# A two-layer vision transformer tower on one core: the random-feature attention computes its angles in row blocks of 32

## The reference, cut to what matters

```python
H, Dh, m = 16, 16, 64
Q, K, V = heads(wq), heads(wk), heads(wv)
def _phi(x, rf, m):
    proj  = einsum('bhtd,md->bhtm', x, rf)
    scale = exp(-sum(x * x) * 0.5) / sqrt(m)
    return concatenate([cos(proj), sin(proj)]) * scale
Qf, Kf = _phi(Q), _phi(K)
KV  = einsum('bhnd,bhnv->bhdv', Kf, V)
QKV = einsum('bhnd,bhdv->bhnv', Qf, KV)
Z   = maximum(Qf . sum(Kf), 1e-06)
h = h + (QKV / Z) @ wo.T
```

## Time and profile before

| | |
|---|---|
| median of three runs | 464.89 us (464.15 to 467.36) |
| the profiled execution | 466.66 us, span 464.8 us |
| TensorE busy (PE) | 377.4 us, 81% |
| VectorE (DVE) | 238.3 us, 51% |
| GpSimd (POOL) | 184.2 us, 40% |
| ScalarE (ACT) | 171.3 us, 37% |
| mean granted clock of TensorE | 0.899 |

### The profile page before, as it was taken

One profiled execution on the slowest core, in us unless ns is written; L12 is line 12 of the kernel. 1 busy time (PEld: TensorE's weight loads), 2 busy tenths in 40 slices (PEclk: granted clock), 3 DMA queues, 4 the chain that ended last, 5 costly groups with the idle time before them and its releaser, 6 DMA issues.

```text
span 464.8 us, 9446 instructions
## 1 busy us (share of the span) xinstructions
PE 377.4 (81%) x3380; PEld 319.6 (69%) x3380; DVE 238.3 (51%) x798; ACT 171.3 (37%) x403; POOL 184.2 (40%) x97
## 2 busy tenths in 40 slices
PE   5999999988169999999707999999983199999930
PEld 4878888876159898999607758777772187887730
DVE  2834434352425455555336054577867267676713
ACT  1264343430113434353302565554421145345410
POOL 0016510101250989999063900012114117687524
PEclk9999999995559999999956999999995589999985
DMA  8999200000016878883525000000000147887313
GB/s 303 414 430 420 93 11 13 13 12 24 19 31 223 301 284 301 292 300 114 198 69 204 1 0 1 1 1 23 1 23 11 62 114 260 271 269 240 121 32 119
DMA packets 16352, 65.34 MB, mean 141 GB/s; under 512 B 2880, under 2 KB 8512, under 8 KB 11584
## 3 DMA queue, kind: packets, MB, share of 16 engines
q1 hardware_dynamic: 14784, 60.72, 35.8%
q0 software_dynamic: 1536, 4.20, 2.9%
HBM read 55.21 MB, written 9.70 MB: 140 GB/s over the span
## 4 chain that ended last, share of the span: by engine, by line
PE 69%; ACT 8%; issue 7%; DVE 7%; DMA 5%; POOL 2%; SPq 0%; POOLq 0%; DVEq 0%; ACTq 0%
PE ps L695 10%; PE ps L697 9%; PE ps L696 9%; PE ps L1102 7%; PE ps L422 7%; PE ps L1113 3%; PE ps L455 3%; PE ps L1288 3%; PE ps L1125 3%; PE ps L475 2%; PE ps L1099 2%; PE ps L985 2%; POOL area_y L553 2%; ACT ps L508 2%; PE ps L598 1%
## 5 line engine op out<-in xcount | busy, mean ns | idle before, releaser
L695 PE MATMUL ps<-xeT,wslot 128*128 128x160 bf16 x384 | 84.2, 240 | 7.1 <-DVE xeT L760 3.3
L696 PE MATMUL ps<-xeT,wslot 128*128 128x160 bf16 x384 | 83.8, 239 | 0.0
L878 POOL TENSOR_TENSOR area_q<-wslot 128x4096 bf16<-128x4096 f32 x8 | 56.4, 7054 | 36.0 <-DMA wslot<-blob_dram 36.0
L884 POOL TENSOR_TENSOR area_w<-wslot 128x2048 bf16<-128x2048 f32 x16 | 57.6, 3602 | 10.9 <-DMA wslot<-blob_dram 10.9
L697 PE MATMUL ps<-xeT,area_q 128*128 128x160 bf16 x256 | 55.1, 238 | 0.0
L695 PE MATMUL ps<-hid,wslot 128*128 128x160 bf16 x256 | 53.7, 233 | 0.0
L697 PE MATMUL ps<-hid,area_w 128*128 128x160 bf16 x256 | 53.6, 233 | 0.0
L696 PE MATMUL ps<-hid,wslot 128*128 128x160 bf16 x256 | 53.5, 233 | 0.0
L695 PEld LDWEIGHTS ps<-xeT,wslot 128*128 128x128 bf16 x384 | 38.7, 101 | 13.8 <-issue 6.1
L772 DVE TENSOR_TENSOR hid<-ps,hid 128x160 bf16<-128x160 f32 x128 | 39.7, 316 | 1.1
L878 POOL TENSOR_TENSOR area_w<-wslot 128x2048 bf16<-128x2048 f32 x8 | 28.8, 3602 | 28.1 <-DMA wslot<-blob_dram 20.1
(11 more groups left out here) (169 smaller groups left out, 806.8 us busy)
## 6 DMA issues: line engine op xcount, KB each, us to landing
wslot<-blob_dram SPq DMA_DIRECT2D x8, 2048.0 KB, 7.7
wslot<-blob_dram SPq DMA_DIRECT2D x16, 1024.0 KB, 5.7
wslot<-blob_dram SPq DMA_DIRECT2D x8, 1031.0 KB, 5.2
slots_dram<-hid SPq DMA_DIRECT2D x8, 544.0 KB, 14.0
xe<-slots_dram SPq DMA_DIRECT2D x16, 128.0 KB, 2.1
slots_dram<-ye SPq DMA_DIRECT2D x16, 128.0 KB, 4.8
area_x<-x_dram SPq DMA_DIRECT2D x4, 384.0 KB, 6.3
area_w<-wq_dram SPq DMA_DIRECT2D x1, 1024.0 KB, 9.2
```

Of the source, the lines that this page charges most:

```text
L695: nc.tensor.matmul(out, w_high[:, s, high_at:high_at + P], x_high, start=first, stop=False)
L696: nc.tensor.matmul(out, w_high[:, s, high_at:high_at + P], x_low, start=False, stop=False)
L878: nc.gpsimd.tensor_tensor(w_low1[L][:, s, :], wslot[:, s, 0:SECOND[L]], w_high[:, s, 0:SECOND[L]], ALU.subtract).then_inc(main[L].low1_rea ...
L884: nc.gpsimd.tensor_tensor(w_low2[:, s, :], wslot[:, s, o:o + KF * D], w_high[:, s, o:o + KF * D], ALU.subtract).then_inc(main[L].low2_read ...
```

## The change

- The angles of eight heads (four `angles` steps) are computed by one group on TensorE: four blocks of 32 rows, each with two heads of 16 rows, each into its own bank (`F_BANK` = 1, 2, 6, 4). `rfs` has two places instead of eight. The quarter turn is a matmul of 32 rows with 1/32 of the value. The group waits until all earlier angle banks are taken. ScalarE and VectorE work per bank as before.
- Bank 4 now holds angles, so `kernel` has bank 3 alone and waits for the mask of the step before.
- ScalarE runs a small `Exp` once the first tile of the second attention is normed, and a small `Sin` right ahead of its first rounding copy.
- For tiles 0 and 1 (`EARLY`) VectorE keeps only the statistics of the `norm` step. `refine` and `norm_apply` run on GpSimd, and so does the scaling into `xin`.

```diff
+HT = 2
-        rfs = sb("rfs", [P, HC, P])
+        rfs = sb("rfs", [P, HT, P])
-        quarter = sb("quarter", [1, P], BF16)
-        ones_row = sb("ones_row", [1, 4 * P], BF16)
+        quarter = sb("quarter", [P, P], BF16)
+        ones_row = sb("ones_row", [P, 4 * P], BF16)
+        early = sb("early", [P, 2])
+        outer_guess = sem("outer_guess")
+        EARLY = NT - 2
...
         def project1_act(act):
+            act.wait_ge(ln_done[2], 1)
+            nc.scalar.activation(early[:, 0:1], const[:, C_ONE:C_ONE + 1], ACT.Exp)
...
-        F_BANK = (1, 2, 6)
+        F_BANK = (1, 2, 6, 4)
+        A_BANK = 3
+        QUARTERS = 4
...
                 if step == "angles":
                     t, j = n // 8, n % 8
-                    if n >= 3:
-                        pe.wait_ge(F_taken, n - 2)
-                    nc.tensor.matmul(ps[:, F_BANK[n % 3], :], quarter[:], ones_row[:], start=True, stop=False)
-                    for a in range(2):
-                        hd = 2 * j + a
-                        mm = nc.tensor.matmul(ps[:, F_BANK[n % 3], a * 2 * P:(a + 1) * 2 * P], rfs[:, hd % HC, :],
-                                              qkT1[:, t, hd // HC, :, :], start=False, stop=(a == 1))
-                    mm.then_inc(F_full, 1)
+                    if n % QUARTERS:
+                        continue
+
+                    if n:
+                        pe.wait_ge(F_taken, n)
+                    parts = [(F_BANK[b], slice(b * HT * DH1, (b + 1) * HT * DH1)) for b in range(QUARTERS)]
+                    for bank, r in parts:
+                        nc.tensor.matmul(ps[:, bank, :], quarter[r, :], ones_row[r, :], start=True, stop=False)
+                    for a in range(HT):
+                        for bank, r in parts:
+                            mm = nc.tensor.matmul(ps[:, bank, a * 2 * P:(a + 1) * 2 * P], rfs[r, a, :],
+                                                  qkT1[r, t, j // 4, :, :], start=False, stop=(a == 1))
+                            if a == 1:
+                                mm.then_inc(F_full, 1)
                 elif step == "kernel":
...
-                    if n >= 2:
-                        pe.wait_ge(A_taken, n - 1)
+                    if n:
+                        pe.wait_ge(A_taken, n)
...
         def attn1_act(act):
+            nc.scalar.activation(early[:, 1:2], const[:, C_BEFORE:C_BEFORE + 1], ACT.Sin)
...
                 elif step == "norm":
                     dve.wait_ge(wo_taken[1], n + 1)
-                    norm_tile(dve, st, n, h, xn, ln_done[3])
+                    if n < EARLY:
+                        norm_stats(dve, st, n, h, outer_guess)
+                    else:
+                        norm_tile(dve, st, n, h, xn, ln_done[3])
...
-                elif step == "xin":
-                    dve.wait_ge(rstd_ready, n + 1)
-                    norm_apply(dve, n, xn, xin, xin_ready)
+                elif step == "xin" and n >= EARLY:
+                    dve.wait_ge(rstd_ready, n - EARLY + 1)
+                    norm_apply(nc.vector, n, xn, xin, xin_ready)
...
             for t in range(NT):
+                if t < EARLY:
+                    pool.wait_ge(outer_guess, t + 1)
+                    refine(nc.gpsimd, newton[:, 1, :], own.step, t, own.step)
+                    norm_apply(nc.gpsimd, t, h, xn, ln_done[3])
                 pool.wait_ge(inner_guess, t + 1)
-                refine(nc.gpsimd, newton[:, 1, :], own.step, t, lambda ins: ins.then_inc(rstd_ready, 1))
+                if t < EARLY:
+                    refine(nc.gpsimd, newton[:, 1, :], own.step, t, own.step)
+                    norm_apply(nc.gpsimd, t, xn, xin, xin_ready)
+                else:
+                    refine(nc.gpsimd, newton[:, 1, :], own.step, t, lambda ins: ins.then_inc(rstd_ready, 1))
...
-            nc.vector.memset(quarter[:, FEAT:P], 0.25).then_inc(quarter_ready, 1)
+            nc.vector.memset(quarter[:, FEAT:P], 0.25 / (HT * DH1)).then_inc(quarter_ready, 1)
```

More of the change, by code:

```diff
@@ L120, in build @@
         w1 = sb("w1", [P, 4, KD, D])
-        rfb = sb("rfb", [P, HC, P])
-        rfs = sb("rfs", [P, HC, P])
+        rfb = sb("rfb", [P, HT, P])
+        rfs = sb("rfs", [P, HT, P])
         wslot = sb("wslot", [P, 2, W0])
@@ L234, in norm_stats, with norm_apply @@
                                     float(RSQRT_MAGIC), ALU.mult, ALU.add).then_inc(ready, 1)
-        def norm_apply(dve, t, src, dst, done):
-            nc.vector.tensor_scalar(dst[:, t, :], src[:, t, :], mv[:, t, 0:1], rstd[:, t:t + 1],
-                                    ALU.subtract, ALU.mult).then_inc(done, 1)
+        def norm_apply(eng, t, src, dst, done):
+            eng.tensor_scalar(dst[:, t, :], src[:, t, :], mv[:, t, 0:1], rstd[:, t:t + 1],
+                              ALU.subtract, ALU.mult).then_inc(done, 1)
         def refine(eng, work, step, t, done):
@@ L256, in norm_tile @@
             refine(nc.vector, newton[:, 0, :], st.step, t, st.step)
-            norm_apply(dve, t, src, dst, done)
+            norm_apply(nc.vector, t, src, dst, done)
         ln_done = [sem(f"ln_done{n}") for n in range(4)]
@@ L1031, in norm2_dve @@
                 for t in range(first, first + 2):
-                    norm_apply(dve, t, h, xn, ln_done[2])
+                    norm_apply(nc.vector, t, h, xn, ln_done[2])
         def values1_dve(dve, st):
@@ L1109, in attn1_pe @@
                     pe.wait_ge(feat_ready, 2 * n + 2)
-                    if n >= 2:
-                        pe.wait_ge(A_taken, n - 1)
+                    if n:
+                        pe.wait_ge(A_taken, n)
                     for a in range(4):
-                        mm = nc.tensor.matmul(ps[:, 3 + n % 2, a * P:(a + 1) * P], feat[:, 4 * g + a, 1, :],
+                        mm = nc.tensor.matmul(ps[:, A_BANK, a * P:(a + 1) * P], feat[:, 4 * g + a, 1, :],
                                               feat[:, 4 * g + a, 0, :], start=True, stop=True)
@@ L1159, in attn1_act @@
                         act.wait_ge(feat_ready, n - 2)
-                    nc.scalar.activation(vt[:, n % 3, :], ps[:, F_BANK[n % 3], :], ACT.Identity,
+                    nc.scalar.activation(vt[:, n % 3, :], ps[:, F_BANK[n % 4], :], ACT.Identity,
                                          bias=const[:, C_ROUND:C_ROUND + 1]).then_inc(whole_ready, 1)
@@ L1180, in attn1_dve @@
                     dve.wait_ge(whole_ready, n + 1)
-                    nc.vector.scalar_tensor_tensor(vt[:, n % 3, :], vt[:, n % 3, :], ROUND, ps[:, F_BANK[n % 3], :],
+                    nc.vector.scalar_tensor_tensor(vt[:, n % 3, :], vt[:, n % 3, :], ROUND, ps[:, F_BANK[n % 4], :],
                                                    ALU.subtract, ALU.subtract).then_inc(F_taken, 1)
@@ L1186, in attn1_dve @@
                         dve.wait_ge(av_done, n - 1)
-                    nc.vector.tensor_tensor(am[:, n % 2, :, :], ps[:, 3 + n % 2, :].rearrange("p (a n) -> p a n", a=4),
+                    nc.vector.tensor_tensor(am[:, n % 2, :, :], ps[:, A_BANK, :].rearrange("p (a n) -> p a n", a=4),
                                             image, ALU.mult).then_inc(A_taken, 1)
@@ L1356 @@
     patches = patches.reshape(NT, P, KP, P).transpose(3, 0, 2, 1).reshape(P, NT, KP * P)
-    rf = np.zeros((P, HC, P), np.float32)
+    rf = np.zeros((P, HT, P), np.float32)
     for j in range(HC):
         for twice in range(2):
-            rf[j * DH1:(j + 1) * DH1, j, twice * FEAT:(twice + 1) * FEAT] = np.asarray(L1_attn_rf).T
+            rf[j * DH1:(j + 1) * DH1, j % HT, twice * FEAT:(twice + 1) * FEAT] = np.asarray(L1_attn_rf).T
     arrays = {
```

## The result

The changed kernel takes 474.91 us in the median (472.29 to 475.58), the kernel before 464.89: the ratio is 1.018, 95% interval 1.013 to 1.023. It is slower; 459.8 was predicted, with 468 as the upper end. Medians here are of all executions of a kernel, but every ratio leaves out executions over 1.5% above the fastest of their kernel, so that it can differ a little from the ratio of the medians.

What follows compares the result with a forecast made beforehand. TensorE's matmuls were taken to bound the second attention; 10.5 us gained at full clock less 5.4 lost to the clock gave 5.1 net, from the median of 464.89 to 459.8 us, range 453.5 to 468.

Steps and rivals of the forecast that it cites:

- The clock takes part of it back: Second attention and tail: TensorE's clock falls at the two waits for GpSimd, taking 5.4 of the 10.5 us gained.
- My walk: Walk along the engine queues through the eight angle groups of the second attention, summed at full clock to 64.05 us.
- 5.0 of 6.4 us in the plain groups: TensorE's work within each plain angle group; full clock was expected in groups 1 and 2.
- In a stretch without pauses it rises again: TensorE's clock recovers under unbroken work, read from a mean of 0.79 at 114 to 116 us.
- my term: The clock's predicted cost: 2.2 us each in groups 5 and 7 and 1 in the tail, 5.4 together.
- The slower rival: Low clock sets in with group 3 and never rises: 4.5 us slower, 469.4 us; chance 0.13.
- a cold group leaves TensorE hardly a pause: Argument against the slower rival: at the lower clock a group has 10.5 us of TensorE work, which is the bound.
- About nothing: Worth of moving the norms to GpSimd: 2.5 us Newton steps and 0.6 scaling there, against 2.07 on VectorE.
- G = 1.4: TensorE's time in us for the angles of eight heads, four row blocks at once; bounds 1.25 and 5.5.
- The chain of one group: Group of four angle steps, TensorE through ScalarE's copies to VectorE's last subtraction: 6.4 us, against 9.1 before.
- The divide's place: Group 3, where VectorE's divide of 1.25 us is queued between subtractions: the group takes 7.35 us.
- the tables: ScalarE's early Exp and Sin table loads: about 1 us gained together, all in group 0.

Runs made afterwards that it cites:

- the set g: One of four sets of kernels, each on one chip beside the kernel before; the changed kernel took 473.17 there against 465.1, ratio 1.014.
- The two filled kernels: Changed kernel with useless matmuls in TensorE's pauses, norms of two tiles on GpSimd (461.62 us) or all on VectorE (455.35), against 467.21 for the kernel before.
- the filled kernel with them on GpSimd: Changed kernel plus useless matmuls in TensorE's pauses, norms of tiles 0 and 1 on GpSimd: 461.62 us, ratio 0.989 to the kernel before; first measured 460.32, 0.987.
- the filled kernel with norms on VectorE: Changed kernel plus useless matmuls in TensorE's pauses, all norms on VectorE: 455.35 us, ratio 0.977 to the kernel before; first measured 455.0, 0.980.

## Why the prediction was wrong

**The step that failed is "The clock takes part of it back"**: "full clock in groups 1 and 2 and a fall at each of the two long waits", 5.4 us. Three things in it were wrong.
- The first fall. My walk gave group 0 a length but did not ask what TensorE does in it. It idles 4.39 us and the clock is down before group 1. This is shown by the kernel with the first pause filled (groups 0 to 2: 19.0 us instead of 22.2).
- The pauses inside groups, "5.0 of 6.4 us in the plain groups", were taken as harmless because the clock had held once where TensorE was at work 1.51 of 2 us. The clock fell again behind 290, in group 3, before any wait for GpSimd, in both executions of the changed kernel that were profiled. With the first pause filled it fell there too, at a wait of 1.48 us for the `divide`.
- "In a stretch without pauses it rises again". It rose four times (full again from 276, 284, 300 and 320), but not always: from 332 to 348 the view has TensorE busy 16.00 of 16 us and the clock at 0.50 all along. The rise at 114 to 116 is no promise. As the clock stayed down there, the tail lost 3.7 us and not 1.

What it came to: the full-clock stage of the changed kernel would be an estimated 68.2 us (67.0 measured with norms on VectorE and the full clock, and group 4 longer by 0.9 and group 5 shorter by 0.3 with GpSimd, twice); it took 83.8 and 86.9. So the clock cost an estimated 15.6 and 18.7 us, about three times my term. The slower rival named this mechanism and put it at 15 us and 469.4, with 0.13; of the cases it is the one that came nearest, though it had the clock full up to group 3 and down for good from there, and the trace has it down before group 1 and up four times in between. It deserved more than 0.13, and my upper end of 468 left it out. Its argument against itself, "a cold group leaves TensorE hardly a pause", is true in the trace and didn't help.

**What else the sum missed.** Profile against profile the change is 5.6 us slower; the medians say 10.0, and 8.1 in the set g. The profiled execution of the changed kernel (472.29) is the fastest of its five, and that of the kernel before (466.66) is above its median. The changed kernel's executions also differ in where the clock falls (stages of 83.8 and 86.9), so one profile stands for them badly.

**Norms on GpSimd.** "About nothing" was wrong. The scaling took 1.25 us and not 0.6, outside the bound of 0.9 that I drew from doubling a rate: the subtraction of 2048 columns was no neighbour of an operation with two per-row operands. By its length alone the edit is still small, about 0.6 us per tile at full clock (10.4 + 8.1 against 9.5 + 8.5 for groups 4 and 5). What it costs comes with the pause of 3.7 us that it opens in TensorE. With the norms back on VectorE the pause is 2.0 us, the stage 80.5 instead of 83.8 and 86.9, and the ratio 0.998 instead of 1.014 and 1.018 (in other sets): level instead of slower, 1.6 to 2.0%. In the kernel before, where the pause is 1 us and the clock holds, the same edit costs 2.3 us in the stage. The two filled kernels differ by 6.3 us in the median and 4.3 in the stage, but not by the norms alone: the one with norms on GpSimd leaves the wait for the `divide` of tile 2 unfilled and loses its clock there, with 2.2 of the 4.3 us behind the last sine. So their difference is no price of the norms; some 1.2 of it is.

**Right.** The blocks overlap: 1.29 us at full clock for G = 1.4. (The prediction's 0.216 for a pass of 256 columns does not come out of its rows: 1.06 less 0.10, by four, is 0.24, and its sum then 1.34 instead of 1.25. G = 1.4 covers both.) The Trainium skill, TensorE: Matmul & The Clock Gate, Part 3 (measured speedup), has 3.07 times for four row blocks of 512 columns, by which G would have been an estimated 1.7. Here 16 records of 256 columns take 1.03 us where four take 1.06, about four times, and the measurement decides. The chain of one group: 6.0 us for 6.4 (copies 1.09 apart, as taken). The divide's place: 7.4 for 7.35. Groups 5 and 7 at full clock: 8.1 to 8.6 for 8.6. The whole walk is 64.05 us, at full clock and with norms on GpSimd. At full clock throughout 62.5 were measured with norms on VectorE, by which GpSimd's would make an estimated 63.7; the filled kernel with them on GpSimd took 66.2, with falls of the clock in it. That the filled kernel with norms on VectorE took 64.2 is luck: 1.7 of it is one fall of the clock in group 6 (11.2 us for 9.5). In group 4 the walk's own steps add up to 7.8 and 10.2 where it has 7.9 and 10.1, which changes nothing. The first copy started at 267.46 for 267.4, and the tables are worth 1.1 us of the stage for about 1. The single bank for `kernel` shows in no wait of the filled kernels.

The same page of the Trainium skill (Part 1, a second HAM failure mode) speaks of a clock that swings in a bf16 kernel whose matmul groups cycle through PSUM banks with small idle times, at a cost in throughput. The windows above (0.62 and 0.53 from 268, 0.68 from 280, 1.00 from 284, 0.60 from 292) agree with it. I had cited it and gave it no weight of its own in the chances.

## What to carry to other kernels

When a change frees the engine whose clock depends on its being busy, walk that engine's idle time through every step as carefully as its work, the first one too, and price each pause at what the following stretch costs at the lower level; do not count on the clock to come back. Then try the change together with useless matmuls in its pauses: here they turned 1.4 to 1.8% slower into 1.1 to 1.3% faster, and with the norms left on the faster engine into 2.0 to 2.3% faster. Filling one pause is not enough where others are left: in two kernels here the clock fell at the next unfilled one, of 1.48 and 1.13 us. And a step between two pieces of TensorE's queue was better left here on the engine that does it soonest, VectorE, although that is the busier one.

## What the runs showed of the hardware that I had not expected

- Four fp32 blocks of 32 rows into four banks cost the same as two (1.03 and 1.02 us) and the return to 128-row matmuls shows no cost: the next one starts 0.96 us behind the first of the 16 records.
- A granted clock of 0.50 with TensorE busy 30.00 of 30 us by the view (two blocks at a time, 275 to 305). The ends of matmuls are modelled there, so this may hide idle time that the view can't show; what the chip counts stays open.
- Two kernels with the same matmuls up to 305 us had TensorE at work 8.78 and 8.77 us of the 10 from 305 on, and clocks of 0.83 and 1.00 there. The busy share of such a stretch alone doesn't tell the clock.
- The start of the stage moved between 261 and 268 us in kernels whose queues are alike up to it, but for the early `Exp`. Spans can therefore differ by several us for reasons ahead of any edit; stages are to be compared from their own start.
